# Eight context products moved to later rounds of the first layer, and batch 0's gate steps spread out, in a two-layer decoder on one core

## What is computed

```python
x = _layernorm(x + _L0_attn_ref(x, ...), axis=-1)
x = _layernorm(x + _L0_xattn_ref(x, ctx_768, ...), axis=-1)
x = _layernorm(x + _L0_ffn_ref(x, ...), axis=-1)
x = _layernorm(x + _L1_attn_ref(x, ...), axis=-1)
x = _layernorm(x + _L1_xattn_ref(x, ctx_768, ...), axis=-1)
x = _layernorm(x + _L1_ffn_ref(x, ...), axis=-1)
...
k = (context @ Wk).reshape(b, m, HEADS, DIM_HEAD)    # in _L1_xattn_ref
v = (context @ Wv).reshape(b, m, HEADS, DIM_HEAD)
...
activation = jnp.sqrt(jax.nn.softplus(logits))       # in _L1_ffn_ref: the gates
top_vals, top_idx = jax.lax.top_k(activation, K)
```

## Time and profile before

| | us |
|---|---|
| median of 3 runs | 1213.0 |
| lowest, highest | 1210.13, 1213.84 |
| profiled execution, its own time | 1211.98 |
| its span, first to last instruction | 1210.2 |
| PE busy (share of the span) | 1094.6 (90%) |
| DVE busy | 744.2 (61%) |
| ACT busy | 550.9 (46%) |
| POOL busy | 111.0 (9%) |
| mean granted clock of TensorE | 0.965 |

### The profile page before, as it was taken

How to read it: one execution, slowest core, us unless ns; L and a number is a source line. 1 busy time by engine, 2 the same in 40 slices (tenths; PEclk the granted TensorE clock), 3 DMA queues, 4 the chain that set the end, 5 groups by cost and what they waited for, 6 DMA issues and landing times.

```text
span 1210.2 us, 19630 instructions
## 1 busy us (share of the span) xinstructions
PE 1094.6 (90%) x7306; PEld 692.0 (57%) x7306; DVE 744.2 (61%) x1092; ACT 550.9 (46%) x1044; POOL 111.0 (9%) x133
## 2 busy tenths in 40 slices
PE   5999997788788988789989999999999999989997
PEld 3443353432222322268766777877777887768664
DVE  3431265679989998553326566465666776866257
ACT  2434333145445555832125566356644554555320
POOL 2011023020200000010001000010002000120020
PEclk9999997679989999899999999999999999989999
DMA  5514311020000000000035333123522633120001
GB/s 156 162 70 149 122 36 40 1 96 14 14 14 14 7 9 1 1 19 1 1 70 144 70 71 71 36 53 89 114 62 70 150 94 83 44 61 2 1 1 35
DMA packets 56493, 67.89 MB, mean 56 GB/s; under 512 B 14665, under 2 KB 35922, under 8 KB 56402
## 3 DMA queue, kind: packets, MB, share of 16 engines
q1 hardware_dynamic: 55234, 65.06, 20.5%
q10 hardware_dynamic: 1168, 1.57, 0.4%
HBM read 30.96 MB, written 13.63 MB: 37 GB/s over the span
## 4 chain that ended last, share of the span: by engine, by line
PE 72%; DVE 14%; issue 5%; ACT 4%; SPq 2%; DMA 2%; POOL 1%; ACTq 0%; DVEq 0%; POOLq 0%
PE p_ring L1723 11%; PE p_unit L1723 11%; PE p_out L1870 9%; PE p_ring L1767 8%; PE p_ring L1847 8%; PE p_ring L1744 6%; PE p_out L1836 5%; DVE halves L1494 5%; PE p_ring L1813 5%; DVE prob_a L1508 2%; PE p_ring L1791 2%; DVE x L1693 2%; PE p_unit L1948 1%; ACT prob_b L1294 1%; PE p_unit L1902 1%
## 5 line engine op out<-in xcount | busy, mean ns | idle before, releaser
L1308 ACT ACTIVATE prob_a<-p_ring 128x1024 f32<-128x1024 f32 x128 | 130.5, 1023 | 113.6 <-PE p_ring L1813 113.2
L1473 DVE TENSOR_REDUCE nmax<-p_ring 128x2 f32<-128x1024 f32 (+1 forms) x128 | 156.0, 1220 | 30.1 <-PE p_ring L1767 30.1
L1294 ACT ACTIVATE prob_b<-p_ring,nmax 128x512 f32<-128x512 f32 (+1 forms) x192 | 158.7, 837 | 32.5 <-DVE nmax L1473 32.1
L1326 ACT ACTIVATE probT_b<-p_ring 128x512 f32<-128x512 f32 x144 | 84.6, 599 | 195.3 <-PE p_ring L1847 193.7
L1494 DVE TENSOR_REDUCE halves<-p_ring 128x2 f32<-128x1024 f32 x128 | 155.6, 1219 | 26.7 <-PE p_ring L1791 26.2
L1767 PE MATMUL p_ring<-stacks 128*128 128x512 f32 x512 | 152.4, 420 | 9.5 <-ACT prob_b L1294 5.4
L1527 DVE COPY probT_b<-p_ring 128x512 f32<-128x512 f32 x112 | 77.1, 688 | 118.3 <-PE p_ring L1847 117.9
L1847 PE MATMUL p_ring<-ident,prob_b 128*128 128x128 f32 x1024 | 136.0, 276 | 4.8 <-DVE probT_b L1527 4.4
L1847 PEld LDWEIGHTS p_ring<-ident,prob_b 128*128 128x128 f32 x1024 | 117.3, 142 | 28.5 <-issue 20.1
L1813 PE MATMUL p_ring<-x_q,x_kq 32*128 32x512 f32 x512 | 120.1, 660 | 1.9 <-DVE halves L1494 1.6
L1494 DVE TENSOR_REDUCE wide_max<-p_ring 128x2 f32<-128x256 f32 (+3 forms) x64 | 52.6, 823 | 95.5 <-PE p_ring L1785 95.3
(11 more groups left out here) (208 smaller groups left out, 1536.9 us busy)
## 6 DMA issues: line engine op xcount, KB each, us to landing
stacks<-splitH_b SPq DMA_DIRECT2D x80, 128.0 KB, 2.3
stacks<-splitL_b SPq DMA_DIRECT2D x80, 128.0 KB, 2.4
stacks<-x_kd SPq DMA_DIRECT2D x32, 256.0 KB, 4.7
x_kd<-early SPq DMA_DIRECT2D x8, 512.0 KB, 3.1
x_v<-x_vd SPq DMA_DIRECT2D x8, 512.0 KB, 3.9
x_vd<-early SPq DMA_DIRECT2D x6, 512.0 KB, 2.8
a_st<-a_image SPq DMA_DIRECT2D x32, 64.0 KB, 2.8
x_kd<-xT SPq DMA_DIRECT2D x4, 512.0 KB, 3.1
```

The source lines that it names most:

```text
L1294: ins = nc.scalar.activation(prob_b[:, n % NP_SLOTS, a * 512:a * 512 + w_all], p_scores[:, n % 2, a * 512:a * 512 + w_all], ACT.Exp, bias= ...
L1308: nc.scalar.activation(prob_place(key), slot_of("S2", key), ACT.Exp, accum_out=x0_sums[:, m:m + 1]).then_inc(done["E2"], 1)
L1473: nc.vector.tensor_reduce(nmax[:, n % 4, 0:heads], src, AX.X, ALU.max, negate=True).then_inc(done["M"], 1)
```

## The change

```diff
--- before.py
+++ after.py
@@ -424,7 +424,8 @@
         vals = [("v", "X1", b, j) for b in range(B) for j in range(NKV // 256)]
         order = [u for both in zip(vals, keys) for u in both]
         order = [u[1][1:] for u in x0_keys(1)] + order
-        return [unit(*u, at=24, after=[UA("v", "A0", 1, 1), UA("cT", 3, 1)]) for u in order]
+        return [unit(*u, at=24 if n < 10 else 66 + 3 * (n - 10), after=[UA("v", "A0", 1, 1), UA("cT", 3, 1)])
+                for n, u in enumerate(order)]
 
     last_one = prob_items(PAIRS[-1])[-1]
 
@@ -504,8 +505,9 @@
 
     def gates(b):
 
-        return [step("ZD", b, 0, after=[UD("mr", b)]), step("ZA", b, 0), step("ZD", b, 1), step("ZP", b),
-                step("ZD", b, 2, after=[("ZP", (b,))])]
+        apart = starts(21) if b == 0 else 0
+        return [step("ZD", b, 0, after=[UD("mr", b)]), step("ZA", b, 0), step("ZD", b, 1, at=apart and apart + 9), step("ZP", b),
+                step("ZD", b, 2, at=apart and apart + 13, after=[("ZP", (b,))])]
 
     def hidden(b):
 
```

## The result

| | before | after |
|---|---|---|
| median of 4 runs, us | 1212.25 | 1193.99 |
| lowest, highest | 1210.13, 1213.84 | 1192.41, 1195.28 |
| profiled execution, its span | 1211.98, 1210.2 | 1193.53, 1191.8 |
| mean granted clock | 0.965 | 0.973 |

The change is faster by 18.3 us: ratio 0.985 [0.983, 0.987]. Forecast were 14.5 us. Two repeats of the change, each beside new runs of before, gave 0.985 as well.

A forecast was written before the change was run, and what follows sets the result against it. PE was taken to bound the kernel, busy 90% of the span. The terms -21 + 2 + 11 + 0 - 6.5 = -14.5 us took the median from 1213.0 to 1198.5 us, range 1191 to 1207.

The forecast's parts named there:

- Doubles taken out: Rounds 38 to 47: removing eight doubles of PE work gains 21 us, bounds 18 and 25.6.
- Half clock behind it: A spell at PE's lower clock in the emptied stretch, charged 2 us, bounds 0 and 4.
- The rival without it: PE keeps full clock in the emptied and filled stretches, no charge of 2: 1193.5 us, chance 0.11.
- Seven doubles put in: Rounds 68 to 84: added PE work, partly covered by waits and half clock, costs 11 us, bounds 5.5 and 16.9.
- The eighth, rounds 88 to 92: Double in round 91: 1.8 us longer, 2 given back by fuller clock; sum 0, bounds -3 and +2.
- Gates: Output products of rounds 391 and 393: of 7.3 us lost, 6.5 gained, bounds 4 and 7.3.
- the charge of 0.8: At the gates: DVE has 1.5 us too much work within five rounds, half taken up elsewhere; 0.8 us charged.
- doubles give nothing: Rounds 38 to 92: doubles cost as much in new places as they gave; only gates gain, 1206.5 us, chance 0.14.
- the gates keep their wait: DVE reaches the comparisons before POOL has ended; one us gained there instead of 6.5: 1204 us, chance 0.07.
- Slower: Lower clock stays over rounds 68 to 92, so each added matmul costs double: 1218 us, chance 0.06.
- Full clock in both: PE keeps full clock in the emptied and filled stretches, rounds 88 to 92 give back 3 more: 1193.5 us, chance 0.11.

The follow-up runs named there:

- experiment 4: Kernel before with only the gate edit, ZD 1 and ZP left in rounds 388 and 389, ZD 2 in round 394: 1204.97 us, ratio 0.9945.
- experiment 5: Kernel before with only the gate edit, ZD 1 and ZP in rounds 390 and 391, ZD 2 in round 392: 1207.57 us, ratio 0.995.
- experiment 2: Kernel before with only the eight doubles moved, gates as before: 1201.22 us, ratio 0.991.
- experiment 1: Kernel before with only the gate steps moved, doubles as before: 1204.43 us, ratio 0.994.
- experiment 6: The change, but with its eight doubles close together in rounds 74 to 82: 1203.28 us, ratio 0.992 to the kernel before.
- experiment 8: The change, but with its first two moved doubles in rounds 44 and 47: 1192.97 us, ratio 0.983 to the kernel before.
- experiment 10: The change, but with three doubles in rounds 42, 44 and 47 and five moved: 1197.14 us, ratio 0.986 to the kernel before.
- experiment 7: The change, but with its first two moved doubles left in rounds 38 and 39: 1195.57 us, ratio 0.986 to the kernel before.

## Why the prediction was right

The median came out at 1193.99, inside the range (1191 to 1207), 4.5 us under the forecast. Point by point:

- **Doubles taken out: 21, measured 22.5.** Round 48's scores were due near 129 us; its maximum began at 126.61, of which 1.7 is the earlier start of this execution. The ten emptied rounds took 11.7 us, 1.17 each, between the two bounds (7.5 for nothing but PE's own work, 14.9 at the rate of rounds 69 to 72) and near the 12 that I took. Most of the 1.5 us over is a slip in the sum: the 33.1 us begin at the first double, 0.91 behind round 38's first score (115.98 to 116.89), while the 12 us were for ten whole rounds; from 115.98 on the same sum gives 22.0. The bound of 7.5 was too low: PE is busy for 10.08 us in the emptied stretch.
- **Half clock behind it: 2, measured 2.3 to 3.7.** It came in every profile of the change, for 6.8 or 10.2 us, beginning between 124.8 and 126.9 us, and it fell mostly on rounds 48 to 52. The rival without it falls here.
- **Seven doubles put in: 11, measured 11.1 to 12.4** against the first profile of before (10.7 to 12.1 against the second). The clock (0.96 to 1.00, forecast 0.9 or more), the two waits for POOL, SP's pause (3.0 us of 3.5) and the later cast (5.3 us of 5) came as said. The wait for `normed` was to stay at 2.48; it went to 0.85 with 1.26 for ACT ahead of it, 0.4 less together.
- **The eighth, rounds 88 to 92: 0, measured a small gain at most.** Rounds 88 to 98 took 1.4 to 2.0 us less (profiles of the change against both of before). But the profiles of experiments 4 and 5, which have the doubles where before has them, took 37.7 and 32.7, so this lies within what executions differ by. In the first profile of the change the clock was no better: from 220.36 to 238.72 it is 0.63, where the same rounds of before have 0.68, and PE idles 1.0 us (18.36 - 17.39) instead of 3.3 (19.49 - 16.22). In the two repeats the clock was better, as forecast: 0.81 and 0.79 between the maxima of rounds 88 and 93, where the two profiles of before have 0.68 and 0.54.
- **Gates: 6.5, measured 7.3** in the profile (6.1 against the second profile of before), 0.994 by the runs of the gate steps alone. The margin was 3.5 us (forecast 3.6). The step that failed here is the charge of 0.8 for DVE being 1.5 us over: with `XL`, `ZD` 1, `ZD` 2 and a scaling in five rounds DVE made PE wait for nothing, though it was busy for 5.62 us of 5.65. The charge does exist when the steps stand closer: experiment 5 paid 2.2 for it.

Summed by the middle of the three profiles in each line of the table, against the first of before: -22.5 + 2.5 + 12.3 - 0.1 (rounds 52 to 68) - 1.6 - 7.3 = -16.7 us, beside 16.8 to 18.3 by the medians of the three groups of runs. Over the forecast's 14.5 are 1.5 from the emptied stretch, 1.6 from rounds 88 to 98, 0.8 from the gates; under it 0.5 from the half clock and 1.3 from the filled stretch. No mechanism was missing; these five sizes were off by 0.5 to 1.6. The forecast started from 1213.0, so -16.7 would give 1196.3. The other 2.3 us down to 1193.99 are the spread between groups of runs: before itself came out at 1212.25 here, and the repeats of the change at 1195.5.

One sum of the prediction doesn't come out: with 25.6 gained, 5.5 paid and the other terms as forecast the change is -24.6 us, which is 1188.4 and not 1191. The measured time lies above both.

Of the rivals, "doubles give nothing" was excluded by experiment 2, "the gates keep their wait" by experiments 1 and 4. "Slower" needed a clock under about 0.72 from round 68 to 92, and in the filled stretch it was 0.96 to 1.00. "Full clock in both" was nearly right for the filled stretch and wrong for the emptied one. That case rested beside the rows on the Trainium skill ("TensorE: Matmul & The Clock Gate", section "Loop structure matters more than you think"), whose example of a good loop says of DVE's copy out of PSUM between groups of matmuls that it "doesn't break PE warmth". In that example the next matmuls follow immediately, so it says less of short pauses than I read into it, and for short pauses the trace speaks against it. Windows of after ahead of 124.8 us and behind it:

```profile
114.60:124.80 10.20, 9.13 (x79) 4.67 (x78) 8.33 (x12) 4.83 (x7) 1.85 (x4) 1.00 0.24 77
124.80:135.00 10.20, 10.20 (x52) 4.72 (x50) 4.16 (x6) 2.22 (x3) 1.68 (x3) 0.50 0.10 27
```

The clock is 1.00, then 0.50 for 10.2 us. PE's longest waits ahead of that are these two, of 0.31 and 0.47 us:

```profile
115.22 0.50 PE L1783 MATMUL p_ring<-a_st 32*128 32x512 f32 x2 [0.31 <-ACT xT L1389]
...
122.40 0.44 PE L1783 MATMUL p_ring<-a_st 32*128 32x384 f32 x2 [0.47 <-ACT prob_a L1314]
...
126.50 1.94 PE L1838 MATMUL p_out<-prob_a,a_v 128*32 128x512 f32 x8
```

The last line is an output product of 128x512 x8 that takes 1.94 us; at 187.63 the same took 1.07.

## What to carry to other kernels

- Work that can stand anywhere (here, products that only depend on inputs) belongs where the busiest engine waits for a slower partner, one piece in every few rounds: this gave 1.6 to 1.8 us of cost for each 3.0 us of work, while the same pieces packed one a round starved the partner and cost 2.4. Leaving two of them in the emptied stretch made no difference that the runs show (in one profile, with both in front, the stretch was 3 to 4 us longer).
- When a slow operation on one engine feeds a short one in another's queue, set the distance from the profile (here 5.43 us, and four rounds) and look at what else stands in the reader's queue: 2.2 us of the 7.3 were lost to crowding when the wait itself was nearly gone.
- Profile before and after twice. Two executions of one kernel differed by 4.6 us in span here. For these two the stretches of the table agreed to within 1 us, while the start up to round 10 and the gates differed by 1.4 and 1.2 us.

## What the runs showed of the hardware

- **The clock fell with hardly a wait.** In the emptied stretch PE was busy for 10.08 of 11.15 us with no wait over 0.5 us, and the clock was then at half for 6.8 to 10.2 us, in all three profiles of the change and in those of experiments 2 and 6. In the filled stretch PE was busy for nearly the same share, 40.84 of 44.95 us, with waits up to 1.26 us, and the clock was 1.00 throughout in the first profile; each of the two repeats had 3.4 us at half in it (0.96 over rounds 68 to 88). What differs in the rows is the kind of work: scores with 32 rows, transposes and output products alone in the first, doubles with 128 rows in every third round in the second. Two doubles put back into rounds 44 and 47 (experiment 8, both its profiles) or three (experiment 10) went with a half clock of 3.4 us; two left ahead, in rounds 38 and 39 (experiment 7), with one of 13.6. That where they stood matters is suggested by this, by one profile of the latter. Why the clock fell stays open; no run varied the kind of work alone.
- **The granted clock differs between executions.** Before's half clock behind the gates was 6.8 us in one profile and 3.4 in the other, with nearly the same wait ahead of it (4.43 and 4.61 us).
